# Moving half of the value projection by one step, and the next batch's latents by one step, in an attention and mixture-of-experts kernel

## The reference

```python
latent_kv = x @ w_kv_down                  # 256 -> 128
kv = latent_kv @ w_kv_up                   # 128 -> 2 * 1024, keys and values
q = (x @ w_q).reshape(Bx, Tx, 16, 64)
att = jnp.einsum('bqhd,bkhd->bhqk', q, k) * scale
att = jax.nn.softmax(jnp.where(causal, att, -jnp.inf), axis=-1)
y = jnp.einsum('bhqk,bkhd->bqhd', att, v)
x = layernorm(x + y.reshape(Bx, Tx, 1024) @ w_out)
```

## Time and profile before

| | |
|---|---|
| median of three runs | 3235.69 us |
| the profiled execution | 3234.61 us |
| its span | 3232.7 us |
| TensorE busy | 3118.6 us (96%) |
| VectorE busy | 2066.3 us (64%) |
| ScalarE busy | 1947.1 us (60%) |
| GpSimd busy | 1529.5 us (47%) |
| mean granted TensorE clock | 0.989 of full |

### The profile page before, as it was taken

How to read it: one execution, slowest core, us unless ns; L and a number is a source line. 1 busy time by engine, 2 the same in 40 slices (tenths; PEclk the granted TensorE clock), 3 DMA queues, 4 the chain that set the end, 5 groups by cost and what they waited for, 6 DMA issues and landing times. The chain is left out here.

```text
span 3232.7 us, 62119 instructions
## 1 busy us (share of the span) xinstructions
PE 3118.6 (96%) x20524; PEld 2513.4 (78%) x20524; DVE 2066.3 (64%) x5927; ACT 1947.1 (60%) x4191; POOL 1529.5 (47%) x1616
## 2 busy tenths in 40 slices
PE   6999999999999999999999999989979999999996
PEld 5767777776777777677777777669979999999996
DVE  4666666666667666666666666663878865454445
ACT  5766667676667666666766767655535444444444
POOL 3433334343434334343433434336647777666665
PEclk9999999999999999999999999999989999999998
DMA  4444444454444445444444444447744444443425
GB/s 109 112 115 100 103 119 102 102 124 101 106 102 119 98 102 124 102 111 115 95 105 105 118 115 112 99 136 266 273 143 112 97 105 107 108 101 83 109 51 154
DMA packets 211889, 376.59 MB, mean 116 GB/s; under 512 B 25832, under 2 KB 135784, under 8 KB 211584
## 3 DMA queue, kind: packets, MB, share of 16 engines
q1 hardware_dynamic: 169536, 322.19, 38.4%
q0 software_dynamic: 25152, 33.75, 6.3%
q10 hardware_dynamic: 16896, 16.78, 1.5%
HBM read 129.27 MB, written 75.59 MB: 63 GB/s over the span
## 5 line engine op out<-in xcount | busy, mean ns | idle before, releaser
L215 POOL TENSOR_SCALAR prob<-prob,inv 128x128 f32<-128x128 f32 (+7 forms) x1024 | 775.8, 758 | 1295.2 <-DVE inv L622 1288.4
L617 DVE CUSTOM_DVE_ANT_0 s_ps<-s_ps,mask 128x128 f32<-128x128 f32 (+7 forms) x1024 | 781.9, 764 | 671.0 <-PE s_ps L342 652.8
L510 ACT ACTIVATE prob<-s_ps,neg_max 128x128 f32<-128x128 f32 (+7 forms) x1024 | 759.6, 742 | 347.7 <-DVE neg_max L617 331.9
L341 PE MATMUL s_ps<-k_hh,q_hl 128*128 128x512 f32 (+3 forms) x1536 | 588.8, 384 | 32.7 <-ACT prob L510 21.6
L357 PE MATMUL t_ps<-ident,prob 128*128 128x128 f32 x4096 | 610.6, 274 | 1.0 <-ACT prob_t L600 0.5
L600 ACT ACTIVATE prob_t<-t_ps 128x512 f32<-128x512 f32 (+3 forms) x704 | 376.7, 535 | 280.9 <-PE t_ps L357 274.4
L373 PE MATMUL o_ps<-prob_t,v 128*64 128x512 f32 (+3 forms) x3072 | 537.5, 492 | 1.5 <-DVE y L639 1.5
L357 PEld LDWEIGHTS t_ps<-ident,prob 128*128 128x128 f32 x4096 | 474.9, 140 | 51.6 <-issue 2.8
L342 PE MATMUL s_ps<-k_lz,q_hl 128*128 128x512 f32 (+3 forms) x1536 | 513.3, 346 | 0.0
L341 PEld LDWEIGHTS s_ps<-k_hh,q_hl 128*128 128x128 f32 x1536 | 289.2, 188 | 180.4 <-ACT prob L510 73.8
L373 PEld LDWEIGHTS o_ps<-prob_t,v 128*64 128x64 f32 x3072 | 204.0, 136 | 286.3 <-issue 267.4
(11 more groups left out here) (223 smaller groups left out, 5654.7 us busy)
## 6 DMA issues: line engine op xcount, KB each, us to landing
k_hh<-k_high SPq DMA_DIRECT2D x256, 256.0 KB, 4.2
q_hl<-q_high SPq DMA_DIRECT2D x128, 256.0 KB, 3.9
q_hl<-q_low SPq DMA_DIRECT2D x128, 256.0 KB, 4.2
k_lz<-k_low SPq DMA_DIRECT2D x128, 256.0 KB, 5.2
y_d<-y SPq DMA_DIRECT2D x128, 256.0 KB, 3.0
c_yt<-y_d SPq DMA_DIRECT2D x32, 512.0 KB, 6.8
b_xt<-w SPq DMA_DIRECT2D x16, 1024.0 KB
w_raw<-w SPq DMA_DIRECT2D x16, 1024.0 KB
```

Of the source, the lines that this page charges most:

```text
L215: pool.tensor_scalar(pr, pr, inv[:, s % 4:s % 4 + 1], 1.0, ALU.mult, ALU.mult).then_inc(norm_done, 1)
L341: pe.matmul(out, q_hl[u][h][:, cols], k_hh[u][h][:, w], start=True, stop=False)
L510: act.activation(prob[s % 4][:, 0:(q + 1) * P], s_ps[s % 2][:, 0:(q + 1) * P], ACT.Exp, scale=-1.0, bias=neg_max[:, s % 4:s % 4 + 1], accu ...
L617: dve.tensor_tensor_reduce(part, part, mask[:, T - (q + 1) * P:T], 1.0, -MASKED, ALU.add, ALU.min, neg_max[:, s % 4:s % 4 + 1]).then_inc(m ...
```

## The change

Two numbers in two tables: the second half of the next pair's values is projected in step 10 instead of 9, and the first half of the next batch's latents in step 11 instead of 10. The copies follow by themselves, one step after: the values' from ScalarE's step 10 to 11, the latents' (on ScalarE and VectorE) from 11 to 12.

```diff
-    Q_AT, K_AT, V_AT = (12, 15), (2, 5), (7, 9)
+    Q_AT, K_AT, V_AT = (12, 15), (2, 5), (7, 10)
...
-        L_AT = (10, 14)
+        L_AT = (11, 14)
```

## The result

The changed kernel takes 3243.59 us (11 runs, 3242.47 to 3244.70) against 3235.72 us (11 runs) before: +7.9 us, ratio 1.0025, 95% interval 1.0017 to 1.0032. The forecast was +3.6 us and "same", with 6.5 us as the limit of "same"; the measured move has the sign forecast, is over twice as large, and lies 1.4 us beyond that limit. The time lies inside the stated range of 3233 to 3248. The profiled execution took 3244.70 us with a span of 3242.9.

A forecast was written before the change was run, and what follows sets the result against it. TensorE bounds the kernel (busy 96%), so only its waits can change. Ordinary pairs +2.2 us (56 of -0.03 + 0.07) and seven latent pairs +1.4 give +3.6: 3239.3 us against 3235.69, range 3233 to 3248.

The forecast's parts named there:

- a wait opens at step 10: TensorE, step 10: must wait for step 11's exponential; of 0.81 us taken from step 9, 0.50 return as a new wait.
- VectorE's late copy of step 11's odd chunk: Step 12's transposes: VectorE's copy ends 0.38 us after they begin, costing +0.07 us a pair, bounds nothing to 0.38.
- The even chunk: ScalarE, step 11: its copy now ends at 623.96, reaching step 12's first transposes at 624.10 against 624.24; hidden by 0.14 us.
- the latents wait for the values' copy: Seven pairs with latents, after step 11's transposes: a wait of 0.31 us, with step 12 starting 0.50 us later.
- One of the prediction's own signs of being wrong: Ordinary pair, from one step 9 to the next: the whole is wrong if it doesn't come out 0.04 us longer.
- step 10 with the values: 1.47 plus 0.81: TensorE, ordinary pair: step 10 lasts 1.47 us plus the projection's 0.81, so 2.28, and step 11 starts 0.50 later.
- the prediction's first term: Ordinary pair, steps 9 to 12: old wait at step 12 goes, a new one opens at step 10; -0.03 us.
- the middle between bounds: Each of the seven pairs with latents: cost taken as 0.2 us between bounds 0 and 0.43, together +1.4 us.
- the second latents' wait in step 14: Seven pairs, step 14: the existing 0.36 us wait for the queries' low parts takes up part of the lateness.
- The wait merely moves: Rival: the odd chunk's lateness in step 12 is caught up, total -0.3 us, 3235.4; chance 0.17, within "same".
- Slower: Rival: ScalarE's full queue in step 11 makes the even chunk late too, 0.2 us a pair, 3250.5; chance 0.25.
- Faster: Rival: the new wait in step 10 doesn't open, step 12 starts 0.53 us earlier, 3207; chance 0.08.

The follow-up runs named there:

- the third buffer: Changed kernel with step 12's odd chunk of transposes put in o_ps instead of the t_ps buffer: 3238.58 us against 3234.78 for the kernel before.
- the run with the doubled half: Changed kernel with the eight matmuls of the values' second half done twice in step 10: 3298.38 us against 3235.06 for the kernel before.
- the run with the pieces: Changed kernel with the values' second half projected as two blocks in step 9 and two in step 10: 3223.38 us against 3234.78 before.
- the best run: Changed kernel, ordinary pairs' values split over steps 9 and 10, step 12's odd chunk in o_ps, ScalarE's chunk first, latent pairs' values whole in step 9: 3214.25 us.
- the run with pieces and third buffer: Changed kernel with the values' second half split over steps 9 and 10 and step 12's odd chunk in o_ps: 3223.01 us, ratio 0.9964 to before.

## Why the prediction came out as it did

**Right.** Step 9 falls by 0.31 us, as predicted, and a wait opens at step 10. Step 11 loses its wait (-0.54; predicted -0.53). Step 12 gains 0.06 (predicted +0.07), and the third buffer shows that the cause is the one named: VectorE's late copy of step 11's odd chunk. The even chunk stays hidden. In the seven pairs the latents wait for the values' copy, and step 12 comes 0.51 us later than before (predicted 0.50). That wait is 0.22 us and not 0.31, because step 10 is longer than predicted and the copy's time doesn't depend on that: the latents start 4.20 us after step 10 (786.77, 790.97; predicted 4.18), and the wait took up the error. In ordinary pairs the order of effects, their places and their signs were those of the text.

One of the prediction's own signs of being wrong came true: an ordinary pair was to come out 0.04 us longer, and it came out 0.12 (0.13 in the mean).

**Mis-sized.** The step "step 10 with the values: 1.47 plus 0.81". It grew by 0.92, not 0.81. The 0.81 was the distance from the first of the eight matmuls to the next scores. But the last of a group is followed by the scores after only 0.03 us (624.85 and 624.88 in the changed kernel), and a matmul that follows a transpose starts 0.11 after it. Put in, the group adds eight times 0.111 = 0.89 us; the run with the doubled half measures just that. In step 9 the same 0.08 is saved too, but there it went into the wait, 0.57 us and not 0.50. Of the other 0.03, 0.02 is the start after a wait: the first scores of step 10 are followed by the second after 0.335 us instead of 0.313 (medians), and this is likewise what step 12 was spared; 0.01 has no row. Together it is 0.11 us more in step 10, in an ordinary pair 0.12 or 0.13 instead of 0.04: 56 x 0.09 = 5 us. With the seven pairs 0.6 below their forecast this is 3.6 + 5 - 0.6, about 8, the measured 7.9.

Told as waits: the prediction's first term, -0.03, was a new wait of 0.50 against an old one of 0.53. The new one is 0.58, so the term is +0.05; with the 0.08 of the late chunk that makes the 0.13.

**Left out.** In the seven pairs +0.2 us was the middle between bounds, and that +0.11 came out near it is luck. The prediction let the second latents' wait in step 14 take up part of the lateness. That wait grew instead, from 0.36 to 0.58 us in pair 22. What takes up the lateness is step 12, 0.21 us shorter, and step 13, 0.39 shorter, against 0.20 more in step 14 (the table's L columns). The 0.39 is the wait for the exponential of step 15, which the latents' split on VectorE had caused; the prediction names the split as moved and prices nothing for it. Rows 8 show TensorE's scores only to step 12, so they don't show this wait.

**The rivals.** "The wait merely moves" is half true: it did move, but not for nothing. "Slower" had the right side and the wrong cause here; its queue on ScalarE was real as soon as step 12 started 0.3 us earlier than before, in the run with the pieces. "Faster" is out: the wait in step 10 opened in all 62 pairs before the last two. What the sum kept hidden is that the change is two: the latents' move saves 4.8 us, the values' move costs some 13 (7.3 in the ordinary pairs and 5.5 in the seven), and the second's cost in the seven pairs takes back what the first would have given.

**Not settled.** The 13 us for the values' move is the difference between the whole change and the latents' move. A run with the values moved in the ordinary pairs and the seven pairs left as before was not made; the 6.7 us for the ordinary pairs comes from a run that also has the latents in step 11, though ordinary pairs have none. How much a copy later than 0.39 us costs is not known.

## What to carry to other kernels

When a filler is moved from one wait to another, ask first how long each wait is and how long the filler. Here the filler (0.89 us) was longer than either wait (0.58 and 0.53), and moving it gained nothing; cut in two it filled most of both. Of the 20.6 us of the best run some 16 are from that, with the copies set in the right order, and 4.8 from the latents' move. Take the cost of a group of matmuls from the number times the distance inside the stream, or from the next group's start with and without it, never from its own first start to the next group's. Look also at what moves on the engines that are not busy: a split on VectorE, one step later, gave back a wait on TensorE. And try the parts of a change apart: one of these two was a gain.

## What the runs showed of the hardware

- A 128x128 fp32 matmul row of the values' projection adds 0.111 us to TensorE's stream (eight: 0.89, by doubling them; the code's four matmuls are eight rows), a transpose 0.109 (medians in the pairs' streams), and the scores start 0.03 us after the last of either.
- After a wait for an exponential TensorE's first scores start 0.14 us after the end of that ACTIVATE row, in steps 10 and 12 alike (622.35 to 622.49 in the changed kernel, 623.10 to 623.24 before), and the second scores follow after 0.335 us instead of 0.313.
- TensorE's weight load starts 0.12 us after the end of ScalarE's chunk copy (620.23 to 620.35 in the run with pieces and third buffer) and 0.05 us after the end of VectorE's (medians; 627.86 to 627.92 in the changed kernel).
- A copy by VectorE for which the fifth of seven transposes waits costs nothing when it ends 0.28 us after the first one's start, and 0.08 us when it ends 0.39 after it: the fifth load would start at 0.33 by itself.
- The granted clock was 0.987 to 0.990 in the mean of a run, and 1.00 over the attention's stretch, where the steps were read, in every profiled run. So no step length here is one of clock, but the times scatter with it: the kernel before took 3233.4 to 3234.6 us in its executions at 0.990 and 3235.4 to 3237.6 at 0.988.
